# Start-up loads, a normalisation and idle stretches of TensorE in a two-layer transformer kernel

## The reference

```python
x = LN(x + attention(x))         # 16 heads of 8, rotary, causal
x = LN(x + x + expert(x))        # one of 8 experts by argmax of a gate, 128x128 each
x = LN(x + local_attention(x))   # window of 64 keys, and 25 picked keys:
                                 # out = 0.7 * softmax(window) @ V + 0.3 * softmax(picked) @ V
x = LN(x + mixture(x))           # top 2 of 8 experts, 128 -> 512 -> 128
```

## Time and profile before

| | us |
|---|---|
| median of 3 runs | 1171.98 |
| lowest, highest | 1168.11, 1208.11 |
| profiled execution: time | 1173.57 |
| profiled execution: span | 1171.8 |
| PE / DVE / POOL / ACT busy | 964.1 / 779.2 / 672.6 / 566.5 |

### The profile page before, as it was taken

The page is one execution under the profiler, slowest core; times in us unless marked ns, Lnnn a source line. Parts: engine busy times, 40 slices in busy tenths (PEclk is TensorE's granted clock), DMA queues, the critical chain, the costliest instruction groups (busy, mean ns, idle before and its releaser), DMA issues.

```text
span 1171.8 us, 27686 instructions
## 1 busy us (share of the span) xinstructions
PE 964.1 (82%) x7536; PEld 710.6 (61%) x7536; DVE 779.2 (66%) x3607; ACT 566.5 (48%) x1217; POOL 672.6 (57%) x1508
## 2 busy tenths in 40 slices
PE   0799999999977888599999999999999617999940
PEld 0567777677754444377676766777677416888830
DVE  0467888878853887466677677667767324777736
ACT  0356666666641111145545455545554305777724
POOL 4256666666640222256657687868787640665656
PEclk9889999999986999689999899989998857999975
DMA  6111111111105332211112121212121156788726
GB/s 168 42 30 45 29 46 24 46 42 29 39 3 190 126 126 90 67 27 32 42 47 54 36 54 35 56 35 57 36 54 29 36 145 218 223 249 255 242 83 171
DMA packets 71374, 98.33 MB, mean 84 GB/s; under 512 B 13688, under 2 KB 43256, under 8 KB 71104
## 3 DMA queue, kind: packets, MB, share of 16 engines
q1 hardware_dynamic: 61920, 83.57, 24.5%
q0 software_dynamic: 4992, 10.30, 2.5%
q10 hardware_dynamic: 4352, 3.16, 1.0%
HBM read 49.48 MB, written 24.77 MB: 63 GB/s over the span
## 4 chain that ended last, share of the span: by engine, by line
PE 70%; DVE 11%; issue 6%; POOL 4%; DMA 3%; ACT 3%; SPq 2%; ACTq 0%; DVEq 0%; POOLq 0%
PE bank L342 6%; PE bank L172 5%; PE bank L253 4%; PE bank L351 4%; PE bank L372 4%; PE bank L1477 4%; PE bank L1478 4%; PE bank L1479 4%; PE bank L168 4%; PE bank L406 3%; PE bank L413 3%; PE bank L346 3%; PE bank L381 3%; PE bank L1245 3%; PE bank L398 2%
## 5 line engine op out<-in xcount | busy, mean ns | idle before, releaser
L529 ACT ACTIVATE p<-bank 128x480 f32<-128x480 f32 (+1 forms) x448 | 239.9, 539 | 286.0 <-PE bank L372 115.8
L662 DVE CUSTOM_DVE_ANT_0 bank<-bank,band 128x160 f32<-128x160 f32 x512 | 156.9, 348 | 96.0 <-PE bank L342 94.0
L662 DVE CUSTOM_DVE_ANT_0 bank<-bank,causal 128x128 f32<-128x128 f32 (+1 forms) x512 | 169.9, 388 | 66.0 <-PE bank L346 46.0
L891 POOL TENSOR_SCALAR_AFFINE_SELECT p<-p 128x380 f32<-128x380 f32 (+1 forms) x256 | 146.3, 600 | 85.3 <-ACT p L529 84.4
L662 DVE DVE_READ_ACCUMULATOR2_ANT nm<- 128x1 f32 x1024 | 145.7, 142 | 0.1
L1656 POOL DMA_INDIRECT y_rows<-p,rows x92 | 89.5, 973 | 83.0 <-DVE p L1603 61.4
L342 PE MATMUL bank<-ks,qs 128*128 128x186 f32 x512 | 118.8, 317 | 14.7 <-issue 13.4
L872 POOL TENSOR_SCALAR_AFFINE_SELECT p<-p 128x256 f32<-128x256 f32 (+1 forms) x192 | 90.8, 484 | 68.2 <-ACT p L529 64.7
L342 PEld LDWEIGHTS bank<-ks,qs 128*128 128x128 f32 x512 | 81.8, 201 | 49.2 <-issue 35.8
L372 PE MATMUL bank<-qs,ks 128*128 128x160 f32 x512 | 104.1, 307 | 0.0
L1598 DVE TENSOR_TENSOR ks<-p,ts 128x512 fp32r<-128x512 f32 x92 | 63.9, 694 | 28.3 <-ACT ts L1551 26.7
(11 more groups left out here) (204 smaller groups left out, 2372.9 us busy)
## 6 DMA issues: line engine op xcount, KB each, us to landing
qs<-parts SPq DMA_DIRECT2D x46, 512.0 KB, 5.0
qs<-qf SPq DMA_DIRECT2D x128, 128.0 KB, 2.4
rows<-xr SPq DMA_DIRECT2D x23, 260.0 KB, 3.7
parts<-ks SPq DMA_DIRECT2D x8, 512.0 KB, 2.7
xs<-x_b SPq DMA_DIRECT2D x16, 256.0 KB, 3.1
p<-in_w SPq DMA_DIRECT2D x12, 256.0 KB
xin<-in_x SPq DMA_DIRECT2D x16, 128.0 KB, 2.2
parts<-qf SPq DMA_DIRECT2D x4, 512.0 KB, 2.7
```

The lines of the kernel that those rows point to most:

```text
L529: act.activation(pb[:, :, :].rearrange("p u c -> p (u c)")[:, lo:lo + cols], bank[:, 0:cols], ACT.Exp, scale=SCALE).then_inc(L.exp_done, 1)
L662: return dve.tensor_tensor_reduce(at, at, mask, -1.0, -BIG, ALU.add, ALU.min, nm[:, item:item + 1])
L891: pool.affine_select(out=at, in_=at, compare_op=ALU.is_ge, fill=0.0, base=base, pattern=[[0, 4], [sign, hi - lo]], channel_multiplier=-sig ...
```

## The change

Three parts. **Start:** SP loads `ident`, `w0_qkv`, the two `xin` batches, then `x_a`, then the other constants; ACT issues seven loads of its own; these first nine and not all constants let PE begin (`first_in`). `sel` lands in `x_b` in place of `p`. DVE takes over the memsets of half of `qs`, of `sel`, `pick` and `pick4`; those of `gt`, `ones` and `kg` go behind POOL's part of L0; `vgb` is loaded behind SP's part of L0. A one-off exponential (`warm`) stands ahead of ACT's work. SP waits for `once` and `zeroed` ahead of its first `qs` transfers. **First mixture:** the scaling goes to ACT (`normalise_group`), DVE adds epsilon and forms `shift4` = -mean times the inverse deviation. **Second attention:** four 128x128 products of `ident` with itself into bank `s1[0]`, whose result nobody reads, stand behind `round_kg`. The rest is a merge of semaphores (the last stage's `var_eps` goes into `r_done`) with the same instructions.

```diff
+        def keep_array_busy():
+
+            wait(pe, L.red_done, L.units * (4 * i + 3) + 3)
+            for _ in range(4):
+                pe.matmul(T.s1[0][:, 0:P], T.ident[:], T.ident[:], start=True, stop=True)
...
         if L.local and th.prep:
             round_kg()
+            keep_array_busy()
...
             if x_all_in is not None:
-                dve.wait_ge(x_all_in, 48)
+                dve.wait_ge(x_all_in, 16)
...
             load(0, 0)
             load(1, 1)
+            if behind_first is not None:
+                behind_first()
...
-    wait(dve, M.rstd, 2 * g)
+    wait(dve, M.shifted, g)
     for a in range(G4):
         wait_apart(dve, M.passed, M.stats, G4 * g + a + 1)
         dve.bn_aggr(T.mv4[:, a, :], T.st4[:, a, :]).then_inc(M.aggr, 1)
-
-
-def scale_group(dve, M, T, g, x_to):
-    dve.wait_ge(M.rstd, 2 * g + 2)
+    wait_apart(dve, M.passed, M.aggr, G4 * (g + 1))
+    wait(dve, M.rstd, g)
+    dve.tensor_scalar(T.ve4[:, :], T.mv4[:, :, 1], EPS, None, ALU.add).then_inc(M.sum_done, 1)
+
+
+def shift_group(dve, M, T, g):
+    dve.wait_ge(M.rstd, g + 1)
+    wait(dve, M.x_out, G4 * g)
+    dve.scalar_tensor_tensor(T.shift4[:, :], T.mv4[:, :, 0], -1.0, T.rs4[:, :], ALU.mult,
+                             ALU.mult).then_inc(M.shifted, 1)
+
+
+def normalise_group(act, M, T, g, x_to):
+    wait_apart(act, M.passed, M.shifted, g + 1)
     for a in range(G4):
-        dve.tensor_scalar(x_to[:, bass.ds(G4 * g + a, 1), :], T.sum[:, a:a + 1, :],
-                          T.mv4[:, a, 0:1], T.rs4[:, a:a + 1], ALU.subtract, ALU.mult).then_inc(M.x_out, 1)
+        act.activation(x_to[:, bass.ds(G4 * g + a, 1), :], T.sum[:, a:a + 1, :], ACT.Identity,
+                       scale=T.rs4[:, a:a + 1], bias=T.shift4[:, a:a + 1]).then_inc(M.x_out, 1)
 
 
 def inverse_deviation_group(pool, M, T, g):
-    wait_apart(pool, M.passed, M.aggr, G4 * (g + 1))
+    wait_apart(pool, M.passed, M.sum_done, 2 * g + 2)
     wait_apart(pool, M.passed, M.x_out, G4 * g)
-    pool.tensor_scalar(T.ve4[:, :], T.mv4[:, :, 1], EPS, None, ALU.add).then_inc(M.rstd, 1)
-    pool.wait_ge(M.rstd, 2 * g + 1)
     pool.tensor_tensor(T.rs4[:, :], T.ve4[:, :], T.mhalf[:, :], ALU.pow).then_inc(M.rstd, 1)
...
             keep_gates(act, M, T, g + 1, 1 - p)
+        if has_last(g):
+            normalise_group(act, M, T, g - 1, x_to)
         keep_outputs(g, p)
 
-    groups(act, prologue, body, lambda: None)
-
...
             if e == 7 and has_last(g):
-                scale_group(dve, M, T, g - 1, x_to)
+                shift_group(dve, M, T, g - 1)
...
-        const_in, x_a_in = sem("const_in"), sem("x_a_in")
-        ready, zeroed, preset = sem("ready"), sem("zeroed"), sem("preset")
-        once = sem("once")
-        loads = [(T.ident, "ident"), (T.causal, "causal"), (T.band, "band"), (T.rows, "rows"), (W0.qkv, "w0_qkv"), (T.cos, "cos"), (T.sin, "sin"), (W0.out, "w0_out"),
-                 (T.diag, "diag"), (T.first, "first"), (V0.gate, "gate"), (V0.expert, "expert"), (W1.router, "router"),
-                 (T.tri, "tri"), (T.tok, "tok"), (kidx, "kidx"), (W1.qkv, "w1_qkv"), (W1.out, "w1_out")]
-
-        sel = T.p[0].ap().rearrange("p u c -> p (u c)")[0:E, 0:E * P]
-        rows = [(gi, "gi"), (W1.bqkv, "b1_qkv"), (W1.bo, "bo"), (W1.rb, "rb"), (T.count, "region"),
+        first_in, const_in, x_a_in = sem("first_in"), sem("const_in"), sem("x_a_in")
+        zeroed, once = sem("zeroed"), sem("once")
+        warm = sb("warm", [P, 4])
+
+        sel = x_b.ap().rearrange("p a d -> p (a d)")[0:E, 0:E * P]
+        first_sp = [(T.ident, "ident"), (W0.qkv, "w0_qkv")]
+        first_act = [(T.cos, "cos"), (T.sin, "sin"), (T.causal, "causal"), (W0.out, "w0_out"), (kidx, "kidx")]
+        n_first = 16 * (len(first_sp) + len(first_act) + 2)
+        loads = [(V0.gate, "gate"), (V0.expert, "expert"), (T.first, "first"), (T.band, "band"), (T.rows, "rows"),
+                 (T.diag, "diag"), (W1.router, "router"), (T.tri, "tri"), (T.tok, "tok"), (W1.qkv, "w1_qkv"),
+                 (W1.out, "w1_out")]
+        rows = [(W1.bqkv, "b1_qkv"), (W1.bo, "bo"), (W1.rb, "rb"), (T.count, "region"),
                 (T.region, "region"), (Z.steps, "steps"), (Z.upto, "upto"), (Z.block, "block")]
-        n_const = 16 * (len(loads) + 1 + len(rows))
+        n_const = 16 * (len(loads) + len(rows) + len(T.vgb))
...
-            for t, name in loads:
-                sp.dma_start(t.ap(), a[name]).then_inc(const_in, 16)
-            sp.dma_start(sel, a["sel"]).then_inc(const_in, 16)
-            for t, name in rows:
-                sp.dma_start(t.ap(), a[name].to_broadcast([P, a[name].shape[1]])).then_inc(const_in, 16)
-            sp.dma_start(x_a[:, :, :], x_dram.rearrange("b (a p) d -> p (b a) d", p=P)).then_inc(x_a_in, 16)
+            def other_constants():
+                sp.dma_start(x_a[:, :, :], x_dram.rearrange("b (a p) d -> p (b a) d", p=P)).then_inc(x_a_in, 16)
+                for t, name in loads:
+                    sp.dma_start(t.ap(), a[name]).then_inc(const_in, 16)
+                for t, name in rows:
+                    sp.dma_start(t.ap(), a[name].to_broadcast([P, a[name].shape[1]])).then_inc(const_in, 16)
+                sp.wait_ge(once, 1)
+                sp.wait_ge(zeroed, 5)
+
+            for t, name in first_sp:
+                sp.dma_start(t.ap(), a[name]).then_inc(first_in, 16)
+            attention_sp(sp, L0, T, W0, other_constants)
             for g in T.vgb:
-                sp.dma_start(g.ap(), a["ninth"].rearrange("p (j c) -> p j c", j=4)).then_inc(x_a_in, 16)
-            attention_sp(sp, L0, T, W0)
+                sp.dma_start(g.ap(), a["ninth"].rearrange("p (j c) -> p j c", j=4)).then_inc(const_in, 16)
...
-            pe.wait_ge(const_in, n_const)
-            pe.wait_ge(ready, 3)
-            pe.wait_ge(preset, 4)
+            pe.wait_ge(first_in, n_first)
+            pe.wait_ge(once, 5)
             attention_pe(pe, L0, T, W0)
...
-            act.wait_ge(preset, 4)
-            act.wait_ge(const_in, n_const)
-            act.wait_ge(once, 2)
+            for t, name in first_act:
+                act.dma_start(t.ap(), a[name]).then_inc(first_in, 16)
+            act.dma_start(gi.ap(), a["gi"].to_broadcast([P, NG])).then_inc(first_in, 16)
+            act.dma_start(sel, a["sel"]).then_inc(first_in, 16)
+            act.wait_ge(zeroed, 1)
+            act.activation(warm[:, :], T.mhalf[:, :], ACT.Exp)
+            act.wait_ge(zeroed, 3)
             attention_act(act, L0, T, W0)
             act.wait_ge(L0.pv_done, 4 * B)
-            one_expert_act(act, F0, T, V0)
+            act.wait_ge(zeroed, 11)
+            one_expert_act(act, F0, T, V0, x_a)
...
+            for j in range(4):
+                m = dve.memset(T.qs[1][j][:, :, :].bitcast(F32), 0.0)
+            m.then_inc(once, 1)
+            dve.memset(T.sel[:, :].bitcast(F32), 0.0).then_inc(once, 1)
+            dve.memset(T.pick[:, :, :].bitcast(F32), 0.0).then_inc(once, 1)
+            dve.memset(T.pick4[:, :, :, :], 0.0).then_inc(once, 1)
+            dve.wait_ge(first_in, n_first)
...
+            pool.wait_ge(zeroed, 2)
+            keys = T.ts[:, :, :].rearrange("p a (h c) -> p a h c", c=32)[:, :, 16:32, 24:26]
+            pool.memset(keys, 1.0).then_inc(zeroed, 1)
+            pool.memset(T.mspr[:, :, :, :].bitcast(F32), 0.0).then_inc(zeroed, 1)
+            for j in range(4):
+                m = pool.memset(T.qs[0][j][:, :, :].bitcast(F32), 0.0)
+            m.then_inc(zeroed, 1)
...
             attention_pool(pool, L0, T, W0)
+            for t in T.gt:
+                pool.memset(t[:, :].bitcast(F32), 0.0)
+            pool.memset(T.ones[:], 1.0).then_inc(zeroed, 1)
+            for par in range(2):
+                m = pool.memset(T.kg[par][:, :, :], 0.0)
+            m.then_inc(zeroed, 1)
             mixture_pool(pool, F0, T, V0)
```

65 lines of the change are left out of this document (28 added, 37 removed).

## The result

The changed kernel takes **1136.97 us** (median of 4 runs, 1132.85 to 1138.24), the kernel before in the same comparison 1170.53 (4 runs, 1168.11 to 1208.11). The ratio is 0.9695, with a 95% interval of 0.9667 to 0.9724: faster, by 3.05% (the two medians by themselves lie 33.6 us apart, 0.9713). The profiled execution took 1135.99 us; its span is 1134.2 us, 37.6 less than the 1171.8 of before, at a mean granted clock of 0.920.

What follows compares the result with a forecast made beforehand. The chain of waits was put on PE for 70% of the span and DVE for 11%. 1173.57 - 19.5 - 10.4 - 6.9 = 1136.8 for the profiled execution, forecast median 1136 us (own range 1128 to 1144; with rivals 1122 to 1149).

Steps and rivals of the forecast that it cites:

- The start: Loads split over two queues: first product at 8.3 us, first score product at 22.6 instead of 42.08, 19.5 us gained.
- some 2.4 us: At the start, the time a small transfer was taken to need from its issue to its landing.
- The 10.3: At the start, the us from the first product to the spreading of queries, 11.6 before, which put the spreading at 18.6.
- the upper bound of about 25: Latest forecast time in us for the first score product; the earliest was 21.1, the value taken 22.6.
- The rival of the late loads: Start: first loads share engines with `x_a`, or spreading waits behind it; first product at 12, gain 14 not 19.5; chance 0.13.
- The first attention: No gain forecast; the clock at each stage's start was left as is, some 3 us to both sides by chance.
- The first mixture: Shift replaces DVE's scaling: 1.85 us saved in each of six bodies, 11.1, less 0.7 at the end, 10.4 us gained.
- The shift waits: First mixture: DVE's shift waits for the first `lower_weights` (1.25 us), so the next `xm` begins 1.85 us earlier.
- In a body of 12.3 it does not bind yet: First mixture: PE, busy 11.35 us of a 14.10 us body, would not yet limit a body of 12.3.
- the shift does not wait: 17: Rival, first mixture: the shift runs without waiting, giving 17 less 0.7 in place of 10.4 us, total 1130; chance 0.15.
- The second attention: Products close three long clock dips, 9.5 us, and cost 1.6 plus 1.0: net 6.9 us gained.
- The 0.81 us gap is all the idleness ahead of them: Second attention: PE's wait behind key picking is the only idleness before the dips; reason for taking the full 9.5 us.

Runs made afterwards that it cites:

- the kernel with the input last: Changed kernel with the load of the whole input, `x_a`, moved from the head of SP's later list to its end: 1134.23 us, ratio 0.9649.
- The repetition: The changed kernel run once more, unaltered, on another chip: 1137.37 us, ratio 0.9671.
- the shift on GpSimd: Changed kernel with `x_a` loaded at the end of SP's list and GpSimd instead of VectorE forming the first mixture's shift: 1130.88 us, ratio 0.9621.
- narrow products: Changed kernel with each of the four products behind the key picking streaming 8 columns instead of 128: 1149.56 us, ratio 0.9798.
- the second traces of the scaling back and of the old start: Reruns of the changed kernel with scaling back on VectorE (1155.69 us, 0.9823) and with the former one-queue start (1157.20 us, 0.9808).
- the shift on GpSimd in the first group: Changed kernel, its load order kept, GpSimd forming the shift, on a disturbed chip; only the mixture counts: 78.4 us first to last power, against 80.4.

## Why the prediction was right, and where its steps were not

The forecast of 1136 us and the measured 1136.97 agree, and the profiled sum, -36.8, stands against -37.6. Its three terms held in direction and two of them in size; inside them several misses cancelled. That the sum came so close is partly luck: the 3.25 us that the start fell short were made up by 4.45 us in the first attention, which the forecast had at nothing.

**The start: the term was mis-sized, -16.25 for -19.5.** The step that failed is the path from the first loads to the first score product, at three places. The first product came at 9.59 and not 8.3 (1.3 us): `sel`, the last load on ACT's queue, took 5.6 us to land, where "some 2.4 us" was taken for a small transfer. From there to the issue of the queries it was 11.86 us and not 10.3 (1.6 us). The 10.3 was right, as the kernel with the input last shows (9.82 to 20.28, 10.5), but SP's list was not done: the held issue lasted 8.89 us, not 7, and the first attention was already waiting when the list ended at 21.23. The landing took 4.4 us and not the 4.0 that lie between 18.6 and 22.6 (0.4). Together these are the missing 3.2, but for rounding. The first score product thus lies 0.8 us beyond the upper bound of about 25. `x_a`, which the prediction had done at 11.2, landed at 16.0 (2.87 + 13.1). The rival of the late loads had this mechanism half right: `sel` and the queries did land late while the 16 engines were busy, but the order of `x_a` within the list changes nothing, and its 12 us for the first product were not reached (the eleven traces with these first loads have it between 8.82 and 11.30). The Trainium skill, DMA: Bandwidth & Descriptors, section "Issuing engines are not separate DMA queues", says that transfers of all issuing engines interleave on the same 16 engines; the trace with the input last agrees, with a share of 1.00 and a landing after 4.8 us, where the same transfer took about 2.5 before. It is not the whole reason: in the changed kernel the landing took 4.4 us although the share was 0.28 to 0.30 from 20 to 24 us, and what held it there no run shows. The table load is off the path, at 4.34.

**The first attention: left as is, it gave 4.45.** The prediction allowed 3 us to either side for where the clock's rhythm falls. The stage lasted 307.4 to 310.8 us in all kernels read here but the one with eight products (312.7) and the kernel before (312.2), with the new start and with the old one, so it isn't an effect of the start. The granted clock sets these two apart: both have 13.7 us at 0.50 behind their first score product (36.7 to 50.3, and 52.2 to 65.8). In the changed kernel the like stretch lies at 17.1 to 30.8, so that only 5 us of it fall behind the first score product; the kernels with the old start have 3.4 us there. (The repetition has 12.8 us in two pieces, and 310.4 us.) At 0.48 us for each low microsecond, the prediction's own figure from the earlier trace rows, 8.7 us less give an estimate of 4.2 us, nearly the whole 4.45. Where this stretch falls no edit explains.

**The first mixture: right, -11.2 for -10.4.** The shift waits, as forecast: 1.22 us beside `lower_weights` (L1345), 0.16 us alone. Products resume 2.19 us behind the power's start (425.77 to 427.96), where before it was 4.02 (457.66 to 461.68): 1.83, for the forecast 1.85. From power to power, five of the first six steps are shorter by 1.79 to 1.87; the other gained 3.51, since a short dip at 448.1 to 451.5 of before is gone. That is not chance alone: each of the three traces with the scaling on VectorE has one or two such dips in these bodies, and none of the eleven with it on ScalarE has one between the first power and the seventh. The forecast did not have this gain. The last step and the end cost 1.8 together, where 0.7 was taken; the 1.7 of the dip makes up for it. The Trainium skill, SBUF — State Buffer, section "Who interferes with whom", says that a VectorE instruction with two SBUF inputs contends with a GpSimd instruction that reads SBUF; 1.22 against 0.16 us agrees with it, and with the shift on GpSimd it is gone.

**"In a body of 12.3 it does not bind yet": right, but with nothing to spare.** The first four full bodies came out at 12.24 to 12.39 us, so PE took nothing from the forecast 1.85. But its busy time stayed, 11.35 of 14.10 before and 11.16 of 12.39 after, a share of 0.90, and taking the shift off VectorE as well shortens a full body by 0.1 only. The rival "the shift does not wait: 17" was priced on bodies of 11.3, for which PE has no room: its mechanism, made to happen on GpSimd, was worth 2 us and not 6.

**The second attention: right by a cancelled pair, -7.0 for -6.9.** The products cost nothing, where 2.6 was taken: like iterations take the same in both traces (25.38 and 25.37; 26.97 and 26.97). The three long dips gave 7.0, where 9.5 was taken: the first 3.19 (28.56 to 25.37), the second 2.83, and the third, which lies behind the last key picking, about 1.0. "The 0.81 us gap is all the idleness ahead of them" was right in what to fill and wrong as a reason: narrow products fill it too, and that kernel is no faster than the one without. In the median the products are worth 12.7 us. The mean granted clocks of those runs, 0.898 to 0.919 without the products and 0.917 to 0.930 with them, say that in three of the other five runs without them the clock was low for longer than in the profiled one (0.913); where, no trace shows.

Nor do the products keep every long dip away. Ten traces have four or eight of full width. Leave out the low stretches in which the stage begins and ends; then six of them have none of 6.8 us or more behind the second key picking, and four have (the second traces of the scaling back and of the old start, the shift on GpSimd in the first group, and the eight products). All four traces without products or with narrow ones have such dips. That the products act through the clock is shown by the runs taken together; why they fail in some is open.

**The parts don't add up.** Taking each part out alone costs 12.7 (products), some 15 to 18 (scaling, from the ratios 0.9823 and 0.9671 to 0.9695) and some 13 to 16 us (start, 0.9808), 41 to 47 in all, while the whole gained 34 to 36 in the medians. Each of these ratios has an interval of some 4 to 6 us to either side, so the excess is not clear of noise. In the traces the excess is in stages that the edit doesn't touch, and in one of them it is one long stretch at the low clock. Why such a stretch comes in some runs stays open.

## What to carry to other kernels

Where the clock falls behind a short gap on TensorE, try products of full width in it, as many as the gap holds and none more: four were free, eight cost 0.84 us each time. Judge them by several runs, since one trace may or may not hold a long dip. A small instruction that waits for GpSimd's next long one can be put on GpSimd itself (1.22 us became 0.20); but divide the next engine's busy time by the new length of the loop body first: at a share of 0.90 only 0.1 us of 1.2 was left to gain. In this start the order of the list behind the first loads was worth nothing: wherever the large transfer stood, something behind it waited.

## What the runs showed of the hardware that was not expected

- An 8-column and a 128-column product have nearly the same busy time in the trace (130 and 143 ns per instruction, from 1.04 and 1.14 us for eight), yet the kernel with the wide ones is 12.2 us faster in the median, at a higher granted clock.
- The clock can stay at 0.50 for 24 us in the middle of a stage in which PE is busy throughout (641 to 664 in the kernel with the old start), in a program whose two fastest runs are 9 and 10 us shorter than this one, at a granted clock of 0.927 and 0.925 in place of 0.918.
- Of the loads that follow the 2 MB load in rows of 512 bytes, the first held its queue for 8.89 us, and the next ones took 0.43 each. With the same load at the end of the list none was held.
